# Attention output projection on one Trainium2 core: weights made stationary, the attention result moved in two parts

## What is computed

```python
x = x + 0.5 * _L0_ffn_ref(_layernorm(x), ...)     # linear, tanh
x = x + _L0_attn_ref(_layernorm(x), ...)          # linear attention
x = x + 0.5 * _L0_ffn_ref(_layernorm(x), ...)
x = x + 0.5 * _L1_ffn_ref(_layernorm(x), ...)     # spectral
x = x + _L1_attn_ref(_layernorm(x), Q, K, V, W)   # softmax attention
x = x + 0.5 * _L1_ffn_ref(_layernorm(x), ...)     # spectral

def _L1_attn_ref(x, Q, K, V, W):
    q = einsum('qdh,bcd->bhcq', Q, x) * sq; k = ...; v = einsum('vdh,bcd->bhcv', V, x) * sv
    p = softmax(where(causal, einsum('bhcq,bhCq->bhcC', q, k) / 64, -inf))
    y = einsum('bhcC,bhCv->bhcv', p, v)
    return einsum('dvh,bhcv->bcd', W, y) * (sqrt(128 / 64) / 16)
```

## Time and profile before

| | |
|---|---|
| median of 3 executions | 1265.42 us (1264.5 to 1266.61) |
| the profiled execution | 1264.62 us |
| its span, first to last instruction | 1262.9 us |
| TensorE busy | 1193.1 us (94%), 10883 matmuls |
| VectorE busy | 1025.6 us (81%) |
| ScalarE busy | 1003.5 us (79%) |
| POOL busy | 586.6 us (46%) |
| mean granted TensorE clock | 0.992 |
| bytes moved over the span | 9 GB/s |

### The profile page before, as it was taken

How to read it: one execution, slowest core, us unless ns; L and a number is a source line. 1 busy time by engine, 2 the same in 40 slices (tenths; PEclk the granted TensorE clock), 3 DMA queues, 4 the chain that set the end, 5 groups by cost and what they waited for, 6 DMA issues and landing times.

```text
span 1262.9 us, 38370 instructions
## 1 busy us (share of the span) xinstructions
PE 1193.1 (94%) x10883; PEld 1040.7 (82%) x10883; DVE 1025.6 (81%) x4877; ACT 1003.5 (79%) x3491; POOL 586.6 (46%) x913
## 2 busy tenths in 40 slices
PE   4699977799999999999999999999999999999996
PEld 3588976678888888888888888888888888888885
DVE  6878879977788888888888888888888888888874
ACT  4866648678888888888888888888888888888884
POOL 4821137725444444444444444444444444444442
PEclk9999989999999999999999999999999999999999
DMA  8000000000000000000000000000000000000000
GB/s 222 1 1 0 1 2 1 1 2 2 3 2 9 0 8 7 1 8 0 8 0 8 0 8 0 8 0 8 0 8 0 8 0 8 0 8 0 9 2 18
DMA packets 14444, 11.81 MB, mean 9 GB/s; under 512 B 852, under 2 KB 12664, under 8 KB 14200
## 3 DMA queue, kind: packets, MB, share of 16 engines
q1 hardware_dynamic: 14240, 11.19, 3.3%
q10 hardware_dynamic: 152, 0.00, 0.0%
HBM read 7.00 MB, written 4.19 MB: 9 GB/s over the span
## 4 chain that ended last, share of the span: by engine, by line
PE 85%; DVE 4%; issue 3%; ACT 2%; POOL 2%; DMA 1%; SPq 1%; POOLq 0%; DVEq 0%; ACTq 0%
PE ps L1158 14%; PE ps L1141 13%; PE ps L1167 10%; PE ps L1127 7%; PE ps L1110 7%; PE ps L1123 6%; PE ps L1111 5%; PE ps L1112 5%; PE ps L1149 2%; PE ps L1148 2%; PE ps L1147 2%; PE ps L988 2%; PE ps L1010 1%; POOL rstd L318 1%; PE ps L1183 1%
## 5 line engine op out<-in xcount | busy, mean ns | idle before, releaser
L816 ACT ACTIVATE pr<-ps,neg_max 128x128 f32<-128x128 f32 (+1 forms) x1024 | 424.8, 430 | 110.7 <-DVE neg_max L538 110.7
L333 POOL TENSOR_TENSOR pr<-pr,rinv 128x256 f32<-128x256 f32 x256 | 157.3, 615 | 517.0 <-DVE rinv L546 517.0
L538 DVE CUSTOM_DVE_ANT_0 ps<-ps,mask 128x128 f32<-128x128 f32 (+1 forms) x1024 | 329.4, 389 | 0.5
L335 POOL TENSOR_TENSOR pr<-pr,rinv 128x512 f32<-128x512 f32 x256 | 266.2, 1040 | 0.0
L553 DVE COPY pT<-ps 128x512 f32<-128x512 f32 x256 | 176.1, 688 | 60.1 <-PE ps L1141 58.6
L816 ACT ACTIVATION_READ_ACCUMULATOR pr<-ps,neg_max 128x1 f32 x1024 | 218.0, 213 | 0.0
L1141 PE MATMUL ps<-ident,pr 128*128 128x128 f32 x1536 | 210.2, 273 | 2.5 <-POOL pr L335 1.1
L1141 PEld LDWEIGHTS ps<-ident,pr 128*128 128x128 f32 x1536 | 179.4, 141 | 21.2 <-POOL pr L335 2.6
L1158 PE MATMUL ps<-pT,space 128*64 128x256 f32 (+1 forms) x2048 | 194.9, 332 | 0.7 <-ACT pT L825 0.5
L1158 PEld LDWEIGHTS ps<-pT,space 128*64 128x64 f32 x2048 | 126.8, 136 | 55.5 <-ACT pT L825 0.7
L1110 PE MATMUL ps<-x_hi,wqk_hi 128*128 128x256 f32 x512 | 168.0, 328 | 2.4 <-issue 1.9
(11 more groups left out here) (188 smaller groups left out, 2637.0 us busy)
## 6 DMA issues: line engine op xcount, KB each, us to landing
out<-x_all SPq DMA_DIRECT2D x16, 256.0 KB, 2.3
x_all<-L_attn_x SPq DMA_DIRECT2D x1, 768.0 KB, 7.0
x_all<-L_attn_x SPq DMA_DIRECT2D x1, 512.0 KB, 5.0
space<-L_attn_Q SPq DMA_DIRECT2D x1, 512.0 KB, 15.2
space<-L_attn_K SPq DMA_DIRECT2D x1, 512.0 KB, 9.4
space<-L_attn_V SPq DMA_DIRECT2D x1, 512.0 KB, 11.1
space<-L_attn_W SPq DMA_DIRECT2D x1, 512.0 KB, 11.5
dft_s<-dft SPq DMA_DIRECT2D x1, 192.0 KB, 2.7
```

The lines of the kernel that those rows point to most:

```text
L333: nc.gpsimd.tensor_tensor(pr[:, buf, :, 0, :], pr[:, buf, :, 0, :], r[:, :, 0:1].to_broadcast([P, 2, P]), ALU.mult)
L335: nc.gpsimd.tensor_tensor(pr[:, buf, :, 1:3, :].rearrange("p h b k -> p h (b k)"), pr[:, buf, :, 1:3, :].rearrange("p h b k -> p h (b k)") ...
L538: last = nc.vector.tensor_tensor_reduce(o, o, mask[:, T - w:T], -1.0, -MASKED, ALU.add, ALU.min, neg_max[:, j, 2 * h + qt:2 * h + qt + 1])
L816: last = nc.scalar.activation(dst, ps[:, BANK_S + 2 * j + h, qt * P:qt * P + w], ACT.Exp, bias=neg_max[:, j, at:at + 1], scale=-1.0, accum ...
```

## The change

The projection's weights become the stationary operand, and y of 256 tokens moves. Both are split in a high and a low part in fp32r, and three products of 256 columns for each pair take the place of two float32 steps of 128. The 24 products of a batch stand in turns 3, 4 and 5 as 9, 9 and 6. The sum then has outputs in its rows: ScalarE copies it to SBUF (`o_out`), and TensorE transposes it back in two transposes (`out_transpose`), in turn 5 behind the transposes of the probabilities; `spectral_product` moves behind them.

y's parts are made as follows. `y_out` copies `BANK_Y` to `y_raw` (one copy of 512 columns in all cases; it was two of 256 in every second batch's first call). `y_high`, on ScalarE behind `probs_T`, casts `y_raw` to `y_hi`. `y_low`, on POOL behind `scale_probs` of the next even turn, makes `y_raw - y_hi`. Each is done four times a batch. The low part of the weights is made once, by VectorE, in the setup (`w_low`), and TensorE waits for it there. `probs_T(n, 0)` of VectorE moves ahead of `add_z` and `add_spectral`. Several buffers share storage with others of earlier stages; `wz_lo` is a view of `xl_lo`, `y_raw` one of `phq`.

```diff
+        def y_places(jb, p):
+            at = jb * PAIRS + p - 1
+            if at > 0:
+                return [(slice((at - 1) * T, (at + 1) * T), slice(0, 2 * T))]
+            return [(slice((2 * PAIRS - 1) * T, 2 * PAIRS * T), slice(0, T)), (slice(0, T), slice(T, 2 * T))]
...
+            def y_low(b, jb, p, calls):
+                pool.wait_ge(yhi_ready, count(calls))
+                if p == 1 and above_0(b - 1):
+                    pool.wait_ge(o_done, count(b - 1))
+                for to, at in y_places(jb, p):
+                    last = nc.gpsimd.tensor_tensor(y_lo[:, to], y_raw[:, (p + 1) // 2 % 2, at], y_hi[:, to].bitcast(F32), ALU.subtract)
+                last.then_inc(ylo_ready, 1)
...
+                    if p == 0 and not first:
+                        y_low(b - 1, 1 - jb, PAIRS - 3, b * (PAIRS // 2) - 1)
+                    if p == 2 and not first:
+                        y_low(b - 1, 1 - jb, PAIRS - 1, b * (PAIRS // 2))
+                    if p == 4 or p == 6:
+                        y_low(b, jb, p - 3, b * (PAIRS // 2) + (p // 2 - 1))
...
+            def w_low():
+                for i in range(2):
+                    dve.wait_ge(su_hi, count(6 + i + 1))
+                    nc.vector.scalar_tensor_tensor(out=wz_lo[:, 4 * i:4 * i + 4, :].rearrange("p h d -> p (h d)"), in0=ps[:, W_BANKS[i], :],
...
+                    probs_T(n, 0)
                     if p + 1 == W_TURN + 2 and not first:
                         add_z(b - 1)
                         if above_0(b - 1):
                             add_spectral(b - 2, b)
-                    probs_T(n, 0)
...
+            def y_out(b, p, calls):
                 act.wait_ge(pv_done, count(b * PAIRS + p))
+                if above_0(calls - 2):
+                    act.wait_ge(ylo_ready, count(calls - 2))
+                nc.scalar.copy(y_raw[:, (p + 1) // 2 % 2, :], ps[:, BANK_Y, :]).then_inc(y_ready, 1)
+            def y_high(b, jb, p, calls, first=False):
+                act.wait_ge(y_ready, count(calls))
...
+                for to, at in places:
+                    last = nc.scalar.copy(y_hi[:, to], y_raw[:, (p + 1) // 2 % 2, at])
+                last.then_inc(yhi_ready, 1)
...
+            def o_out(b):
+                act.wait_ge(o_done, count(b + 1))
+                nc.scalar.copy(oT[:], ps[:, BANK_X, 0:T]).then_inc(o_ready, 1)
...
                         qk_high_odd(n + 3)
+                    if p + 1 == W_TURN + 2 and not first:
+                        o_out(b - 1)
                     exp_head(n + 1, 1, 1, pr_of(p + 1))
...
                     probs_T(n, 0)
+                    if p > 0:
+                        y_high(b, jb, p - 1, b * (PAIRS // 2) + p // 2, first)
...
-            def project_out(b, j, steps, only=False):
-                pe.wait_ge(y_ready, count(PAIRS // 2 * (b + 1) + 1))
...
+            def project_out(b, j, pairs):
+                calls = PAIRS // 2 * (b + 1)
+                for p in range(*pairs):
+                    if p in (0, 3, 5, 7):
+                        pe.wait_ge(ylo_ready, count(calls + (-2, -1, 0, 1)[(0, 3, 5, 7).index(p)]))
+                    of_pair = slice((j * PAIRS + p) * T, (j * PAIRS + p + 1) * T)
+                    mm(ps[:, BANK_X, 0:T], wz_hi[:, p, :], y_hi[:, of_pair], start=(p == 0), stop=False, skip_group_check=True)
+                    mm(ps[:, BANK_X, 0:T], wz_hi[:, p, :], y_lo[:, of_pair], start=False, stop=False, skip_group_check=True)
+                    last = mm(ps[:, BANK_X, 0:T], wz_lo[:, p, :], y_hi[:, of_pair], start=False, stop=(p == PAIRS - 1), skip_group_check=True)
...
+            def out_transpose(b, only=False):
+                pe.wait_ge(o_ready, count(b + 1))
+                for t in range(BT):
+                    last = tr(ps[:, BANK_X, t * D:(t + 1) * D], oT[:, t * P:(t + 1) * P], ident[:])
...
-            pe.wait_ge(su_ev, 6)
+            pe.wait_ge(su_lo, 7)
             qk_product(0, 0, 0, 0)
```

More of the change, by code:

```diff
@@ L163, in build @@
         th = sb("th", [P, 2, GW])
-        xl_hi = sb("xl_hi", [P, 2, GW], F32R); xl_lo = sb("xl_lo", [P, 2, GW], F32R)
-        eq = sb("eq", [P, GW]); rq = sb("rq", [P, GW]); ek = sb("ek", [P, GT, P])
-        phq = sb("phq", [P, 2, GW]); phk = sb("phk", [P, GT, P])
+        xl_hi = y_hi[:, 0:2 * GW].rearrange("p (i n) -> p i n", i=2)
+        xl_lo = sb("xl_lo", [P, 2, GW], F32R)
+        pr = sb("pr", [P, 3, 2, 3, P])
+        eq = pr[:, 0].rearrange("p e k q -> p (e k q)")[:, 0:GW]; rq = pr[:, 1].rearrange("p e k q -> p (e k q)")[:, 0:GW]
+        phk = pr[:, 2].rearrange("p e k q -> p (e k) q")[:, 0:GT, :]
+        phq = sb("phq", [P, 2, GW])
+        pT = sb("pT", [P, 2, 2, 3, P])
+        ek, y0, yT0 = (pT.rearrange("p i e k q -> p (i e k) q")[:, GT * i:GT * (i + 1), :] for i in range(3))
+        yT0 = yT0.rearrange("p t n -> p (t n)")
         vones = sb("vones", [P, GT, P + 1])
@@ L361, in _ @@
             batches(pool, batch)
+            y_low(B - 1, 1, PAIRS - 3, B * (PAIRS // 2) - 1)
+            y_low(B - 1, 1, PAIRS - 1, B * (PAIRS // 2))
+            pool.wait_ge(yhi_ready, B * (PAIRS // 2) + 1)
+            nc.gpsimd.tensor_tensor(y_lo[:, (2 * PAIRS - 1) * T:], y_raw[:, 1, 0:T], y_hi[:, (2 * PAIRS - 1) * T:].bitcast(F32),
+                                    ALU.subtract).then_inc(ylo_ready, 1)
             z_inv_std(B - 1)
@@ L873, in batch @@
                     if p > 0:
-                        y_out(b, jb, p - 1, first)
+                        y_out(b, p - 1, b * (PAIRS // 2) + p // 2)
                     elif not first:
-                        y_out(b - 1, 1 - jb, PAIRS - 1)
+                        y_out(b - 1, PAIRS - 1, b * (PAIRS // 2))
                     if not (last and p == PAIRS - 2):
@@ L895, in batch @@
                     probs_T(n, 0)
+                    if p > 0:
+                        y_high(b, jb, p - 1, b * (PAIRS // 2) + p // 2, first)
+                    elif not first:
+                        y_high(b - 1, 1 - jb, PAIRS - 1, b * (PAIRS // 2))
                     if not (last and p == PAIRS - 2):
@@ L900, in _ @@
             batches(act, batch)
-            y_out(B - 1, 1, PAIRS - 1)
+            y_out(B - 1, PAIRS - 1, B * (PAIRS // 2))
+            y_high(B - 1, 1, PAIRS - 1, B * (PAIRS // 2))
             z_xT_out(B - 2)
@@ L1161, in products @@
                 last.then_inc(pv_done, 1)
-            def project_out(b, j, steps, only=False):
-                pe.wait_ge(y_ready, count(PAIRS // 2 * (b + 1) + 1))
-                for k in range(*steps):
-                    t, p = k // PAIRS, k % PAIRS
-                    last = mm(ps[:, BANK_X, t * D:(t + 1) * D], yT[:, j, p, t * P:(t + 1) * P], wz[:, p, :],
-                              start=(p == 0), stop=(p == PAIRS - 1), skip_group_check=True)
-                if (only or not above_0(b)) and steps[1] == BT * PAIRS:
+            def project_out(b, j, pairs):
[7 more added lines that the diff above has]
+                    last = mm(ps[:, BANK_X, 0:T], wz_lo[:, p, :], y_hi[:, of_pair], start=False, stop=(p == PAIRS - 1), skip_group_check=True)
+                if pairs[1] == PAIRS:
+                    last.then_inc(o_done, 1)
+            def out_transpose(b, only=False):
+                pe.wait_ge(o_ready, count(b + 1))
+                for t in range(BT):
+                    last = tr(ps[:, BANK_X, t * D:(t + 1) * D], oT[:, t * P:(t + 1) * P], ident[:])
+                if only or not above_0(b):
                     last.then_inc(w_done, 1)
@@ L1229, in batch @@
                             pe.wait_ge(z_xT_ready, count(b - 1))
-                    if W_TURN <= p < W_TURN + len(W_STEPS) and not first:
-                        project_out(b - 1, 1 - jb, W_STEPS[p - W_TURN])
-                    if p == W_TURN + len(W_STEPS) - 1 and above_0(b - 1):
-                        spectral_product(b - 2)
+                    if W_TURN <= p < W_TURN + len(W_PAIRS) and not first:
+                        project_out(b - 1, 1 - jb, W_PAIRS[p - W_TURN])
                     if p == V_TURN and not last:
@@ L1246, in batch @@
                         probs_transpose(n - 1, 1 - j, pr_of(p - 1), b * (PAIRS // 2) + p // 2)
+                    if p == W_TURN + len(W_PAIRS) - 1 and not first:
+                        out_transpose(b - 1)
+                        if above_0(b - 1):
+                            spectral_product(b - 2)
                     if p % 2 == 1:
@@ L1265, in _ @@
             pe.wait_ge(out_ready, B - 1)
-            project_out(B - 1, 1, (0, BT * PAIRS), only=True)
+            project_out(B - 1, 1, (0, PAIRS))
+            out_transpose(B - 1, only=True)
             spectral_transpose(B - 1)
```

45 lines of the change are left out of this document (23 added, 22 removed).

## The result

The changed kernel takes 1287.05 us (1286.54 to 1288.94, 4 runs) against 1265.14 (1264.5 to 1266.61) for the kernel before in the same comparison: a ratio of 1.017, 95% interval 1.0155 to 1.0186. It is slower by 22 us. The forecast was 1262.0 and the range ended at 1274.0.

What follows compares the result with a forecast made beforehand. TensorE's instruction list bounds the kernel, with no lead over the ScalarE and VectorE chain at turn 3. Loop -3.4 (0.11 over 31 batches), setup +0.7, end -0.5: -3.2 from 1264.62, 1261.4; median said as 1262.0, range 1250 to 1274.

Steps and rivals of the forecast that it cites:

- y_low at 1.04 us: Each POOL subtraction of 512 columns, four a batch, lasts as long as POOL's 512-column product, 1.04 us.
- TensorE's wait for y_low in turn 5: TensorE's last projection pair waits 0 to 0.2 us for the y_low behind turn 4's scaling; 0.05 charged.
- a gain of 0.11 a batch: Net at turn 3: chain early by 0.46 less 0.35 for VectorE's holds; 3.4 us over 31 batches.
- The holds of turns 6 and 0: y_low on POOL holds VectorE's even low part to 0.42 behind its end; 0.2 and 0.15 us lost a batch.
- idle time there in every batch: Sign: TensorE idles 0.3 to 0.4 us for x_lo before the projection of turn 3.
- turns 2 to 5 hide the hold: In turns 2 to 5 VectorE waits long enough for others to hide its later low part; nothing charged.
- TensorE's gain: Projection as 24 products at 0.12 us plus two transposes: 3.66 - 3.07 = 0.59 us saved a batch.
- y_low and oT late on TensorE: TensorE's waits for y_low of the last pair and ScalarE's copy of oT: 0.05 and 0.08 us a batch.
- ScalarE's casts: Four 512-column casts a batch, about 0.6 us long, 0.5 each with overlap, just fit ScalarE's waits for the maxima.
- Setup and end: One more VectorE step ahead of the first q and k products, +0.7 us; shorter last projection, -0.5 us.
- the locks add up: Rival: delays from even low parts of turns 6 and 0 accumulate, turn 3 0.3 later a batch; +9, 1274 us; chance 0.24.
- y_low or oT is late on TensorE: Rival: last pair waits 0.2 to 0.3, oT up to 0.4; 1266 to 1271 us, put at 1268; chance 0.14.

Runs made afterwards that it cites:

- before_even_broadcast: Kernel before plus an unused 512-column POOL product by one broadcast column behind the scaling of every even turn; 1274.96 us, ratio 1.0085.
- before_pool_even_again: Kernel before plus an unused 512-column POOL subtraction behind the scaling of every even turn, run once more; 1288.15 us, ratio 1.0191.
- pool_2_4: Kernel before plus an unused 512-column POOL subtraction behind the scalings of turns 2 and 4 only; 1265.98 us, ratio 0.9998.
- only_turn_4: Changed kernel with y_low in turns 1, 4, 5 and 7, so only turn 4's stays behind an even scaling; 1264.75 us, ratio 0.9987.
- ylow_odd: Changed kernel with every y_low behind the scaling of the odd turns (1, 3, 5, 7) instead of the even ones; 1254.54 us, ratio 0.9916.

## Why the prediction was wrong

**The step that failed** is one size, y_low at 1.04 us. The prediction took it from a row in which the second operand is one broadcast column, and gave no bound for it, although the trace had no POOL instruction of this size with two full operands. It measured 1.289. Those 0.25 us enter the sum three times: in turns 6 and 0, where the runs show each at full price (below), and in TensorE's wait for y_low in turn 5. There 0.05 was charged and 0.31 is what it costs; that y_low at 1.04 would have saved this is worked out only (in the rows of turn 4 above it would have ended at 745.62, before TensorE could start the pair at 745.77). The sum was a gain of 0.11 a batch; 0.11 - 0.75 is a loss of 0.64 (by the terms as measured, 0.48 gained less 0.31 and 0.81: also 0.64), and measured is a loss of 0.67. That these agree so well is in part luck: of the 0.31, 0.07 comes from the two halves of every second batch, which the sum left out. Over 31 batches the 0.75 are 23 us, and 1262.0 + 23 = 1285, against 1287.05.

**The holds of turns 6 and 0.** That VectorE is held there, and the 0.42 behind POOL's end, were right. The way from there to TensorE was not. The prediction took the delay over the masks, the exponentials and the spectral transpose to TensorE's start of turn 3, and expected 0.3 to 0.4 us of idle time there in every batch. By the distance of two starts less 0.12, that idle time is 0.20 and 0.37 in turn (before, 0.11 and 0.37). TensorE waits earlier, for the low parts themselves, at the scores of turns 7 and 1, where they had been 0.39 and 0.19 to 0.40 us ahead. The size came out near all the same: the prediction charged 0.2 + 0.15 = 0.35 with a 1.04 us instruction, `before_even_broadcast` has just that, and a batch of it is 0.28 longer. With 1.29 us it is 0.80 (`before_pool_even_again`), 0.25 more for each of the two turns. That turns 2 to 5 hide the hold on VectorE was right as well (`pool_2_4` for turn 2, the rows of `only_turn_4` for turn 4).

**TensorE's gain** held. In `ylow_odd`, turn 3:

```profile
703.99 0.38 PE L1230 MATMUL ps<-y_hi,wz_hi 128*128 128x256 f32 x1
704.20 0.28 PE L1231 MATMUL ps<-y_lo,wz_hi 128*128 128x256 f32 x1
704.32 0.28 PE L1232 MATMUL ps<-y_hi,xl_lo 128*128 128x256 f32 x1
...
705.03 0.28 PE L1232 MATMUL ps<-y_hi,xl_lo 128*128 128x256 f32 x1
705.15 0.38 PE L1202 MATMUL ps<-ident,pr 128*128 128x128 f32 x2
```

Nine products in 1.16 us, 0.12 each but for a first step of 0.21, which the prediction said would not be paid. Double turns 2 and 4 are 0.29 and 0.20 shorter than before, 0.49 together; the prediction had 0.36 and 0.23, and the first step is what turn 3 lacks. The 109 ns by the Trainium skill (TensorE: Matmul & The Clock Gate, "Wait — 56ns, not 53.3ns?") would have been too good here: the trace shows 120.

**y_low and oT late on TensorE** were put at 0.05 and 0.08 a batch. In `ylow_odd` the transposes of oT start 0.65 behind the first of the six before them, where six take 0.57 in turn 4: 0.08 at most, as charged, and already within the 0.49. y_low in turn 4 costs 0.31 more (`only_turn_4`).

**ScalarE's casts** last 679 ns, not 600, and still lie in its waits for the maxima (23.8 us in 38 waits after, 33.6 before). In `ylow_odd`, where they stand too, TensorE is busy for 299.26 of 300 us, so they cost nothing that shows.

**Setup and end.** The first q and k product starts at 264.33, 0.15 behind the end of VectorE's first low part of the weights, and 1.05 later than before; +0.7 was expected. The first projection starts 2.8 us later. From 260 to 270 us TensorE's granted clock is 0.66 against 0.83. This delay is not a fixed price of the setup: `only_turn_4`, which has the same setup, starts its first projection at 307.05. The last projection takes its 24 products in 2.9 us, as said, but from the 31st projection's start to the end of the span both kernels need about 35 us (35.1 and 35.3), so the -0.5 did not come.

**The rivals.** It went the way of "the locks add up": at turns 6 and 0, past 0.46 a batch, slower. "y_low or oT is late on TensorE" came true beside it. The first had the chance 0.24, and at 1274 it was short by 13 us. The same wrong length went into it and into the range's end; no run holds turn 6 or turn 0 alone, so how much of the second hold comes from the first is not shown.

`ylow_odd` is 31 x 0.48 = 15 us shorter in the loop and 10.7 us in all. Its first two projections start 1.3 and 2.8 us later than before (308.34 against 307.01, 341.95 against 339.15), and the stretch behind the 31st start takes 0.7 more. In part this is the clock: at the entry of the loop, 330 to 335 us, its granted clock is 0.67 on average (between its two levels, 1.2 and 2.4 GHz) where the kernel before has 1.00, and behind the 31st start it is 0.78 from 1230 to 1235, where the kernel before has 1.00 at that stage (1240 to 1245). Why is open: in the 5 us before the first of these, TensorE is busy for 3.06 us, and for 3.08 in the kernel before.

```profile
330.00:335.00 5.00, 4.67 (x23) 4.29 (x24) 2.89 (x6) 2.46 (x8) 1.61 (x2) 0.67 0.02 5
```

## What to carry to other kernels

Before work goes to an idle POOL, look not at its idle time but at which VectorE instructions with two SBUF inputs start while it runs (or from SBUF to SBUF, see the last section); each with two inputs is held to the end of that POOL instruction and some 0.4 us more. Then look how far ahead of its reader the held instruction ends: 0.39 us in turn 7 was too little, more than 1 us in turn 5 enough. Place such work beside VectorE instructions that read PSUM, or cut it into short pieces (this gave back 0.28 of 0.76 us here), and read the hold from the mean duration of VectorE's group, since neither the waits nor the chain show it. And where a duration enters a sum more than once on a path without slack, give it two bounds: here an error of 0.25 us in one instruction makes, by the sum, nearly all of the difference between a small gain and a loss of 22 us.
